# Fused Flamingo block on one core: how the first batch's Q and K are stacked, where its V products run, and which engine makes the ternary weights

## The reference, cut to what matters

```python
# 8 batches, S = 512 rows, D = 512, 16 heads of 32, hidden 2048
x = x + tanh(g_xattn[0]) * xattn(layernorm(x), ctx, ctx)
x = x + tanh(g_ffn[0])   * ffn(layernorm(x))

def xattn(query, key, value):
    Q, K, V = query @ Wq.T + bq, key @ Wk.T + bk, value @ Wv.T + bv     # in heads
    qk = Q @ K.T                                # per head, 512 x 512
    scores = qk / sqrt(32)
    feats = [scores.mean(), scores.max(-1).mean(), var(softmax(scores), -1).mean()]   # per head
    t = exp(clip(mlp(feats)))                   # one temperature per head
    return softmax(qk / (2 * t)) @ V @ Wo.T + bo

def ffn(x):                                     # w1: 2048 x 512, w2: 512 x 2048
    h = gelu(quant_act(x) @ quant_weight(w1).T)
    return quant_act(h) @ quant_weight(w2).T

def quant_weight(w):
    s = mean(abs(w)); return clip(round(w / s), -1, 1) * s              # ternary
```

## Time and profile before

| | |
|---|---|
| median of 3 runs | 1405.53 us (1403.91 to 1407.44) |
| profiled execution | 1404.38 us, of which the span in the trace is 1402.2 us |
| busy share of the span | PE 86%, DVE 79%, ACT 66%, POOL 30% |
| mean granted TensorE clock | 0.939 of full speed |
| body -1 and body 0 (start to the first part B matmul) | 0 to about 192.6 us |

### The profile page before, as it was taken

How to read it: one execution, slowest core, us unless ns; L and a number is a source line. 1 busy time by engine, 2 the same in 40 slices (tenths; PEclk the granted TensorE clock), 3 DMA queues, 4 the chain that set the end, 5 groups by cost and what they waited for, 6 DMA issues and landing times.

```text
span 1402.2 us, 23484 instructions
## 1 busy us (share of the span) xinstructions
PE 1209.3 (86%) x6684; PEld 443.9 (32%) x6684; DVE 1107.2 (79%) x2054; ACT 921.9 (66%) x1527; POOL 422.6 (30%) x399
## 2 busy tenths in 40 slices
PE   5635769999999899999999899998999899869958
PEld 2201311344224432344224431344224431233224
DVE  7297869887898869887898869887898879983246
ACT  5553769664985669664985669664985679645713
POOL 4289374510253114510253114510353101100210
PEclk9857879999999999999999999999999999889979
DMA  8710231102112221102112221102112210001000
GB/s 296 217 60 8 54 83 52 28 20 69 54 47 46 47 78 47 29 18 69 54 46 46 47 78 46 39 17 68 46 47 45 47 61 1 1 1 61 1 0 30
DMA packets 35475, 73.73 MB, mean 53 GB/s; under 512 B 7952, under 2 KB 7952, under 8 KB 34832
## 3 DMA queue, kind: packets, MB, share of 16 engines
q1 hardware_dynamic: 35344, 72.13, 17.9%
HBM read 38.39 MB, written 8.39 MB: 33 GB/s over the span
## 4 chain that ended last, share of the span: by engine, by line
PE 52%; DVE 26%; ACT 9%; issue 9%; POOL 1%; SPq 1%; DMA 1%; DVEq 1%; ACTq 0%; POOLq 0%
PE b_ps L1251 11%; DVE stat L920 7%; DVE nmax L915 5%; PE o_ps L1449 5%; PE o_ps L1251 5%; ACT region L750 5%; PE z_ps L1251 4%; PE o_ps L1291 4%; PE b_ps L1278 4%; PE a_ps L1272 4%; ACT etile L733 3%; PE b_ps L1428 2%; PE z_ps L1449 2%; PE b_ps L1439 2%; PE z_ps L1302 2%
## 5 line engine op out<-in xcount | busy, mean ns | idle before, releaser
L733 ACT ACTIVATE etile<-a_ps,nmax 128x512 f32<-128x512 f32 x512 | 369.6, 733 | 143.1 <-DVE nmax L915 143.0
L915 DVE TENSOR_REDUCE nmax<-a_ps 128x1 f32<-128x512 f32 x512 | 346.3, 678 | 59.6 <-PE a_ps L1272 55.8
L750 ACT ACTIVATE region<-b_ps,inv2t 128x512 f32<-128x512 f32 x512 | 353.3, 758 | 57.8 <-PE b_ps L1278 29.0
L920 DVE BATCH_NORM_STATS2 stat<-etile 128x6 f32<-128x512 f32 x512 | 348.2, 682 | 6.8 <-ACT etile L733 6.8
L1272 PE MATMUL a_ps<-kst,qst 96*128 96x512 f16 x512 | 204.3, 403 | 61.4 <-ACT etile L733 46.5
L1278 PE MATMUL b_ps<-qst,kst 97*128 97x512 f16 x512 | 196.0, 393 | 23.6 <-ACT region L750 16.5
L1291 PE MATMUL o_ps<-region,vbuf 128*32 128x512 f32 x1024 | 140.2, 620 | 8.2 <-ACT region L750 6.3
L1278 PEld LDWEIGHTS b_ps<-qst,kst 97*128 97x128 f16 x512 | 49.3, 97 | 302.2 <-ACT region L750 279.9
L1302 PE MATMUL z_ps<-region,ones 128*32 128x512 f32 x1024 | 137.1, 608 | 8.4 <-DVE region L939 8.4
L653 POOL TENSOR_TENSOR region<-region 128x512 f16<-128x512 f32 x64 | 76.6, 1197 | 219.3 <-ACT region L783 219.1
L609 POOL TENSOR_TENSOR region<-region 128x512 f32<-128x512 f32 x32 | 40.9, 1277 | 312.8 <-DVE region L946 312.8
(11 more groups left out here) (278 smaller groups left out, 1961.4 us busy)
## 6 DMA issues: line engine op xcount, KB each, us to landing
kst<-region SPq DMA_DIRECT2D x96, 128.0 KB, 2.3
qst<-region SPq DMA_DIRECT2D x96, 128.0 KB, 2.3
xres<-in_x_dram SPq DMA_DIRECT2D x8, 1024.0 KB, 6.5
out_dram<-xres SPq DMA_DIRECT2D x32, 256.0 KB, 2.1
cin<-in_ctxT_dram SPq DMA_DIRECT2D x30, 256.0 KB, 2.7
cin<-in_x_dram SPq DMA_DIRECT2D x28, 256.0 KB, 2.7
kst<-in_f1T_dram SPq DMA_DIRECT2D x2, 1024.0 KB, 12.7
qst<-in_f2T_dram SPq DMA_DIRECT2D x2, 1024.0 KB, 10.7
```

Source lines behind the costliest of these rows:

```text
L733: nc.scalar.activation(etile[:, k % E_SLOTS, :], a_ps[k % A_BANKS][:, :], ACT.Exp, bias=nmax[:, slot_of(n), t:t + 1], scale=1.0).then_inc( ...
L750: nc.scalar.activation(probs[:, s % 2, g, :], b_ps[g % 2][:, :], ACT.Exp, scale=inv2t[:, slot:slot + 1]).then_inc(b_exp, 1)
L915: vec.tensor_reduce(nmax[:, slot_of(k // T), k % T:k % T + 1], a_ps[k % A_BANKS][:, :], AX.X, ALU.max, negate=True).then_inc(a_max, 1)
L920: vec.bn_stats(stat[:, slot_of(k // T) * T + k % T, :], etile[:, k % E_SLOTS, :]).then_inc(a_stat, 1)
```

## The change

It replaces `stack` for batch 0 by `stack_first`, which stacks each product by itself; moves V's products of batch 0 from body -1 to the head of body 0, with the first 12 score tiles (`A_FIRST`) between them; takes tanh behind the first two weight conversions on ACT, with the two gate loads earlier on SP and on a semaphore of their own; moves chunk 1 from POOL to DVE; moves the magnitudes of chunks 1, 2 and 3 on ACT behind the copies of V's first three products; moves `weight_hi` and `weight_lo` of Wo later; and takes x's statistics for batch 1 after set 12 and at the third K product.

```diff
-A_PLAN_0 = (28, (3, 3, 3, 3, 0, 0, 0, 0, 3, 3, 3, 3, 3, 3, 3, 3))
-A_HEAD = 4
+A_FIRST = 12
+A_PLAN_0 = (16, (3, 3, 3, 3, 0, 0, 0, 0, 3, 3, 3, 3, 3, 3, 3, 3))
-MAGNITUDES_AT = {0: 2, 1: 3, 2: 6, 3: 4, 5: 5, 9: 7}
-SCALES_AT = {4: 0, 11: 1}
-TERNARY_AT = {5: 2, 7: 3, 13: 6, 14: 4, 15: 5}
-POOL_CHUNKS, DVE_CHUNKS = (0, 1, 7), (2, 3, 6, 4, 5)
+MAGNITUDES_AT = {0: 6, 2: 4, 4: 5, 8: 7}
+SCALES_AT = {0: 0, 10: 1}
+TERNARY_AT = {1: 2, 3: 3, 5: 1, 14: 6}
+POOL_CHUNKS, DVE_CHUNKS = (0, 7), (2, 3, 1, 6, 4, 5)
...
+        def first_tiles(t):
+            return range(A_FIRST * t // T, A_FIRST * (t + 1) // T)
@@ SP
+            def stack_first():
+                sp_waits.wait_ge(bias_step, 1)
+                sp.dma_start(kst[0][SHIFT:SHIFT + 1, :, :].rearrange("o h n -> o (h n)"),
+                             ones16[0:H * T, :]).then_inc(kst_ones, 16)
+                for stage, dst, first in ((stage_k, kst[0], 0), (stage_q, qst[0], C)):
+                    for n in range(C):
+                        sp_waits.wait_ge(qk_lo_done, nth(0, 2 * C, first + n + 1))
+                        for slot, part in enumerate((0, 0, 1) if first == 0 else (0, 1, 0)):
+                            for g in range(G4):
+                                sp.dma_start(dst[slot * DK:(slot + 1) * DK, g * C + n, :],
+                                             stage[g * DK:(g + 1) * DK, part, n, :]).then_inc(qk_first[n], 16)
...
                 if isinstance(i, int) and i == 0:
-                    for n in (2, 3, 4):
+                    for n in (2, 3):
                         load_f(n)
                     load_c(1, 0)
                     load_c(1, 1)
+                    load_f(4)
                     load_f(5)
+                    for n in range(C):
+                        sp_waits.wait_ge(qk_first[n], 16 * 6 * G4)
+                    sp.sem_inc(kst_in, 16 * 3 * G4)
+                    sp.sem_inc(qst_in, 16 * 3 * G4)
                     load_f(7)
                     load_c(1, 2)
                     load_c(1, 3)
...
-                if has_p:
+                if first:
+                    stack_first()
+                elif has_p:
                     stack(i + 1, 1 - par)
@@ POOL
-                    bank_n, before = mm_use(-1, "V", T - 1)
+                    bank_n, before = mm_use(0, "V0", T - 1)
                     pool_waits.wait_ge(mm_full[bank_n], before + 1)
                 if has_p and not first:
                     for c in range(C):
                         split_c(i + 1, c)
-                        if second and c % 2 == 1:
-                            make_ternary(c // 2)
+                if second:
+                    make_ternary(0)
...
                 for n in range(C):
+                    if second and n % 2 == 0:
+                        normalise_x(1, n // 2, from_cin)
+                        split_x(1, n, from_cin)
+                        split_x(1, n + 1, from_cin)
                     if has_p and not (first and n < 2):
                         split_qk(n)
-                    if second and n % 2 == 1:
-                        normalise_x(1, n // 2, from_cin)
-                        split_x(1, n - 1, from_cin)
-                        split_x(1, n, from_cin)
@@ ACT
+            act_waits.wait_ge(gate_in, 32)
+            nc.scalar.activation(tg[:, :], gates[:, :], ACT.Tanh).then_inc(setup_tanh, 1)
...
+                for t in range(T) if isinstance(i, int) and i == 0 else ():
+                    for k in first_tiles(t):
+                        late_exp(0, k)
+                    bank_n, before = mm_use(0, "V0", t)
+                    act_waits.wait_ge(mm_full[bank_n], before + 1)
+                    nc.scalar.activation(vbuf[0][:, t, :], mm_ps[bank_n][:, :], ACT.Copy,
+                                         scale=1.0 / WSCALE).then_inc(mm_free[bank_n], 1)
+                    if t < 3:
+                        magnitudes(t + 1)
...
                 if first:
                     weight_hi(2, "v")
-                    weight_hi(3, "o")
+                    magnitudes(0)
                     act_waits.wait_ge(bq_scaled, 1)
...
                 if first:
-                    magnitudes(0)
-                    magnitudes(1)
-                    v_out()
                     act_waits.wait_ge(small_in, SMALL_LOADS)
-                    nc.scalar.activation(tg[:, :], gates[:, :], ACT.Tanh).then_inc(setup_tanh, 1)
@@ DVE
+                for k in range(A_FIRST) if second else ():
+                    tile_a(0, k)
...
+                    if second and s == 12:
+                        stat_x(1, 0)
...
-                    if second and n % 2 == 0:
-                        stat_x(1, n // 2)
+                    if second and n == 0:
+                        make_ternary(4)
+                    if second and n == 2:
+                        stat_x(1, 1)
+                    if second and n == 3:
+                        make_ternary(5)
@@ PE
             def score_a(b, par, k):
                 slot, t = slot_of(k // T), k % T
                 pe_waits.wait_ge(a_exp, nth(b, H * T, k + 1 - A_BANKS))
+                if isinstance(b, int) and b == 0 and k % (G4 * T) == 0:
+                    pe_waits.wait_ge(qk_first[k // (G4 * T)], 16 * 6 * G4)
...
-                if has_a:
+                if second:
+                    pe_waits.wait_ge(w_lo_done, 3)
+                    pe_waits.wait_ge(bias_step, BIAS_STEPS)
+                    for t in range(T):
+                        rows = slice(t * P, (t + 1) * P)
+                        split_product(take(0, "V0", t), [lambda c, x=x: x(c, rows) for x in c_parts],
+                                      [lambda c, w=w: w["v"][:, c, :] for w in (w_hi, w_lo)],
+                                      [lambda k=k: score_a(0, 0, k) for k in first_tiles(t)], bias=0)
+                if has_a and not second:
```

More of the change, by code:

```diff
@@ L58 @@
 A_BANKS, E_SLOTS, E_LATE, S_LATE = 4, 3, 1, 2
-assert all(sets + sum(dense) == H * T for sets, dense in (A_PLAN_0, A_PLAN, A_PLAN_7))
+assert all(sets + sum(dense) == H * T for sets, dense in (A_PLAN, A_PLAN_7))
+assert A_FIRST + A_PLAN_0[0] + sum(A_PLAN_0[1]) == H * T
 LINKS_NORM, LINKS_W, LINKS_M, LINKS_F = 3 * C, 6, 11, 5 * T
@@ L120, in some @@
         return [(stage, k) for k in range(count)] if present else []
-    uses = some("S", 2, setup == 0) + some("K", C, has_p) + some("W", T, has_b)
+    uses = some("V0", T, setup == 0) + some("S", 2, setup == 0) + some("K", C, has_p) + some("W", T, has_b)
     if setup == 0:
@@ L127, in bank_uses @@
     uses += some("Q", C, has_p)[:2] + some("xq", T, has_b) + some("Q", C, has_p)[2:]
-    uses += some("V", T, has_p and setup == -1)
     uses += some("up0", NB, has_b) + some("up1", NB, has_b)
@@ L331, in flamingo_kernel @@
         kst_ones = sem("kst_ones")
+        gate_in = sem("gate_in")
+        qk_first = [sem(f"qk_first{n}") for n in range(C)]
         x_first, res_in = sem("x_first"), sem("res_in")
@@ L398, in a_plan, with a_start @@
             return {0: A_PLAN_0, 7: A_PLAN_7}[i] if isinstance(i, int) else A_PLAN
+        def a_start(i):
+            return A_FIRST if isinstance(i, int) and i == 0 else 0
+        def first_tiles(t):
+            return range(A_FIRST * t // T, A_FIRST * (t + 1) // T)
         def dense_tiles(i, point):
             sets, dense = a_plan(i)
-            first = sets + sum(dense[:point])
+            first = a_start(i) + sets + sum(dense[:point])
             return range(first, first + dense[point])
@@ L410, in set_tiles @@
             count = sets * (s + 1) // SETS - first
-            return {g: first + n for n, g in enumerate({1: (1,), 2: (0, 2), 3: (0, 1, 2)}[count])}
+            return {g: a_start(i) + first + n for n, g in enumerate({1: (1,), 2: (0, 2), 3: (0, 1, 2)}[count])}
         block = ctx.enter_context(nc.Block())
@@ L449, in stack @@
                     if isinstance(b, int) and b == 1 and first == C:
-                        sp_waits.wait_ge(tern_dve, 5)
+                        sp_waits.wait_ge(tern_dve, 6)
                     if isinstance(b, int) and b == 1 and first == 0:
-                        sp_waits.wait_ge(tern_pool, 2)
-                    if isinstance(b, int) and b <= 1 and first == 0:
-                        sp_waits.wait_ge(bias_step, 1)
+                        sp_waits.wait_ge(tern_pool, 1)
+                        sp_waits.wait_ge(tern_dve, 3)
+                    if isinstance(b, int) and b == 1 and first == 0:
                         sp.dma_start(kst[par][SHIFT:SHIFT + 1, :, :].rearrange("o h n -> o (h n)"),
@@ L530, in _ @@
                 sp.dma_start(bqk[:, 1, :], bk.rearrange("(g p) -> p g", p=P)).then_inc(bqk_in, 16)
+            sp.dma_start(gates[:, 0:1], g_xattn.partition_broadcast(P)).then_inc(gate_in, 16)
+            sp.dma_start(gates[:, 1:2], g_ffn.partition_broadcast(P)).then_inc(gate_in, 16)
             load_w("q", WqT)
@@ L549, in _ @@
             sp_waits.wait_ge(out_done, (B + 1) * 16 * T)
```

(18 more changed lines are left out.)

10 lines of the change are left out of this document (4 added, 6 removed).

## The result

The changed kernel takes 1418.47 us (median of 4 runs, 1417.57 to 1419.27) against 1406.32 us for the kernel before (4 runs); the ratio is 1.0091, 95% interval 1.0077 to 1.0105. It is slower by 12.2 us. The time lies 3.2 us under the 1421.7 us of the prediction, and the change is 5.1 us smaller than the forecast 17.3. Its profiled execution took 1418.13 us, with a span of 1416.3 us, 14.1 more than before.

The account below looks back on a forecast made before the run. DVE was taken to bound batch 0's part A: resumption 93.9 + work 98.4 + idle 4.0 and 2.0 gives 198.3 against 180.97, +17.3 us on 1404.4, so 1421.7 us. Stated range 1407 to 1428.

Parts of the forecast that it names:

- SP's queue: Batch 0 stacking on SP: 96 issues of 32 KB at 0.628 us each, from 25.9 to 86.2 us.
- Rival 1: Cheap issues on SP: 1409.4 us at 0.50 each, 1380 if by bytes; gain 0.10, no change 0.10 shared with another rival.
- First tile: DVE's first maximum, behind K's and Q's first stacking: about 65.8 against 63.64, +2.2 us; early tanh brings nothing.
- The step that decides: Chunk 2's load, behind all 96 issues, lands at 91.4; ACT waits, DVE idles 20 us and resumes at 93.9.
- What DVE had left: DVE's remaining batch 0 work: 102.1 us plus 4.0 for chunk 1, less 7.7 done, 98.4 us.
- Stall for x: DVE's 9.6 us wait for x's third and fourth tiles: gone, taken as 0, with 2 us to spare.
- After the stall, and the turn of x: DVE's later idle time: 2.0 us (0 to 4) after the long wait, 4.0 us kept at x's turn.
- Gate loads: The two gate issues on SP only change places; no cost counted.
- Sum: DVE's last statistics of batch 0 end at 198.3 against 180.97, +17.3 us, passed on whole: 1421.7 us.

Follow-up runs that it names:

- experiments 6 and 10: Kernel before with tanh alone taken early: 6 with gate loads ahead of Wq's, 1407.11 us; 10 with them behind Wo's, 1406.50 us.
- Experiment 1: Changed kernel, loads of chunks 2 and 3 issued between K's and Q's stacking, 4 and 5 behind the second Q product's: 1406.77 us.
- Experiment 3: Changed kernel with the old stacking, K and Q whole in 24 DMAs of 128 KB: 1396.46 us.
- experiment 2: Changed kernel with batch 0's K stacked whole and Q by products, 60 issues instead of 96: 1407.72 us.
- experiment 4: Changed kernel with K stacked whole, Q by products, chunk loads 2 to 5 behind Q's first and second products: 1395.18 us.
- experiment 9: As 8, with gate loads and tanh moved later, ctx's first two parts behind Q's second product, the others ahead of chunk 7: 1386.63 us.
- experiment 5: Changed kernel with ACT's magnitudes of chunks 2 to 7 taken later, scales and ternary chunks following; SP unchanged: 1414.51 us.
- 8: On experiment 4, V's first two products run ahead of the first score: 1391.20 us.
- experiment 7: On experiment 4, chunk 1 back on POOL and chunk 0 back between ctx's second and third parts: 1407.39 us.

## Why the prediction was right

- **SP's queue.** Right. Pitch 0.645 for a forecast 0.628 (range 0.50 to 0.687). The stacking began 4 us sooner (21.95 for 25.9), since chunk 6's issue took 0.43 us and not 3.9; so all was issued at 83.9 for 86.2. Rival 1 is out by the pitch alone. Its low end was misread by a little: the lowest pitch in the trace of before is 0.48 (54.13 to 54.61), not 0.50, which would have put that end of the range 2 us lower.
- **First tile.** 63.03 for 65.8, by the same 4 us less the higher pitch. That tanh taken early brings nothing was right (experiments 6 and 10), the reason only in part: the scores were there at 54.70, so their readiness did not cover the last 8 us of the wait. ACT did, with V's last copy (62.78) and the magnitudes of a chunk ahead of the first exponential (65.26).
- **The step that decides.** ACT stood 15.85 us for chunk 2, between the second V copy and exponential 5; DVE stopped behind maximum 7 and waited 16.40 us. DVE resumed at 91.47 for 93.9. Experiment 1 keeps all 96 issues and moves four loads ahead of part of them; the wait goes and 11.6 us come back, net of a first score 4.2 us later. Experiment 3, with 24 issues again, gets 22.3 back.
- **What DVE had left.** From the resumption to the end 105.2 us for 104.4. Without waits it is 97.4 for 98.4. Chunk 1 took 4.35 us (113.80 to 118.15) for 4.0, but other chunks went faster, so that six cost 22.9 us where five had cost 19.9.
- **Stall for x.** I took 0 with 2 us to spare; it was 1.1. DVE came to the tiles at 151.06 for 155, the tiles landed near 152.1 for 153. So the term was nearly right, but part of this is luck, for the margin is not held by what I had added up. In the kernel after and in experiments 1 to 4 and 9, whose DVE ends lie 32 us apart, POOL came to x 12.6 us before DVE wanted the third tile, each time, and the wait was 1.1 to 1.2. POOL's arrival, after and in experiment 9 (DVE stood for x from 151.06 and from 119.10):

```profile
138.44 0.23 POOL L646 TENSOR_SCALAR rstd<-mv 128x2 f32<-128x2 f32 x1 [0.20 <-POOL f L630]
```
```profile
106.48 0.23 POOL L653 TENSOR_SCALAR rstd<-mv 128x2 f32<-128x2 f32 x1 [0.20 <-POOL f L637]
```

  In all six, DVE's comparison of chunk 6 and the end of POOL's chunk 0 fall together, and both take longer there than elsewhere (DVE's second instruction 2.66 us for 2.35, two of POOL's about 2.5 and 2.6 for 1.57). That this is what keeps the two in step is argued and not shown. Making DVE earlier does not by itself bring the stall back, then; it came back where POOL met it at another place (7.3 us in experiment 5 and 5.9 in 8 at this pair). I had counted chunk 1 as a cost of 4.0 and the x stall as a gain of 9.6, 5.6 in favour of the move. On experiment 4 it is 12 in time (experiment 7), together with chunk 0's place.
- **After the stall, and the turn of x.** 1.35 us (0.45 + 0.20 + 0.70) for 2.0; the turn 5.4 (4.11 and two short ones) for 4.0.
- **Gate loads.** Said to only change places on SP; Wq went out at 8.52 and not at 5.33, and Q's first matmul came at 32.28 for 30.87. In the changed kernel this is hidden, since SP still stacked K until 53.49. What it costs elsewhere is open.
- **Sum.** +15.7 us for +17.3. DVE resumed 2.4 us sooner than said, nearly all of it the earlier end of the issues (83.9 for 86.2), and needed 0.8 more from there, in small terms of both signs. The change in median, +12.2, is smaller than either: 2.1 us of the difference is the clock at the end of the profiled executions, and 1.6 is that the profiled execution of before lay 1.9 us under the median of its four runs and that of after 0.3.

The Trainium skill's "Perfetto Trace Analysis", "DMA Optimizations", says that splitting DMAs may let the whole finish sooner where the DMA engines are generally idle. They were: their mean share from 64 to 84 us, while SP stacked Q, was 0.20. The first score came later all the same with both K and Q split, and sooner only with Q split and K whole: DVE's first maximum was at 63.03 with 96 issues, at 56.61 with the old 24 (experiment 3), at 51.74 with 60 (experiment 2).

## What to carry to other kernels

Splitting a transfer so that its first part is ready sooner must be priced in issues of the queue, and the price falls on everything behind it in program order: list what is queued there, and who waits for it in turn. When such a wait is taken away by moving a step back, look for who waits for that step: experiment 5 took 14 us from one wait and got 6, because the step it moved also clears a buffer that another engine's data stand behind. An engine with a low share can still be the one that is late: what counts is when it can begin and who waits for its last step.

## What the runs showed of the hardware

- An issue on SP cost 0.645 us back to back at 32 KB (96 of them), where 128 KB cost 0.628: no gain from size.
- A 32 KB move inside the chip's memory landed in 1.8 us, but in 5.0 us when 2 MB of loads had been issued just ahead of it (experiment 1, DMA share 0.97).
- Comparisons on DVE and on POOL were longer where they fell together. In the kernel after, chunk 1's second comparison on DVE took 3.12 us and POOL's first of chunk 0 beside it 3.60; elsewhere in the same kernel the same shapes took 2.35 (chunks 2 and 3, POOL idle) and 1.57 (DVE at its tiles). But chunk 4's took 2.35 although POOL was busy beside it, so what else decides is open.
